# Query stage of a Perceiver kernel: two heads' 96-row half blocks packed into three blocks of 128

## The reference

```python
q_hk = (hidden_q @ Wq.T).reshape(Bv, Sv, H, K)
q_big = jnp.einsum('bshk,hkq->bshq', q_hk, w_kc_q)      # 192 channels a head
q_big = _apply_rope(q_big, sin_q, cos_q)                # x * cos + _rotate_half(x) * sin
kv_r = _apply_rope(kv_c, sin_k[None], cos_k[None])
q_r = jnp.einsum('bshq,hqr->bhsr', q_big, W_qr)
k_r = jnp.einsum('bld,hdr->bhlr', kv_r, W_kr)
scores = jnp.einsum('bhsr,bhlr->bhsl', q_r, k_r)
```

## Time and profile before

| | us |
|---|---|
| median of 3 runs (lowest, highest) | 1953.88 (1947.71, 1959.5) |
| the profiled execution | 1954.76 |
| its span, first to last instruction | 1952.6 |
| query stage, first query product to last key product | 38.63 to 257.97 |
| TensorE busy over the span | 1719.2 (88%) |
| VectorE, ScalarE, GpSimd busy | 1164.5, 600.8, 552.0 |

### The profile page before, as it was taken

One profiled execution on the slowest core, in us unless ns is written; L12 is line 12 of the kernel. 1 busy time (PEld: TensorE's weight loads), 2 busy tenths in 40 slices (PEclk: granted clock), 3 DMA queues, 4 the chain that ended last, 5 costly groups with the idle time before them and its releaser, 6 DMA issues. The chain is left out here.

```text
span 1952.6 us, 34931 instructions
## 1 busy us (share of the span) xinstructions
PE 1719.2 (88%) x14360; PEld 1174.4 (60%) x14360; DVE 1164.5 (60%) x1853; ACT 600.8 (31%) x997; POOL 552.0 (28%) x890
## 2 busy tenths in 40 slices
PE   3899968998995548999999999999999877999998
PEld 1333336886784226766776777766677665556555
DVE  4555557678764537676777767776677613443432
ACT  1111114334422313343444333433433311212212
POOL 1100014113211045444445554453554321000000
PEclk9899978999997869999999999998999978999999
DMA  6221120010000111111122111211211113200000
GB/s 200 84 59 47 49 52 1 1 33 12 1 1 3 33 30 31 43 37 39 37 48 47 39 42 36 48 41 35 47 36 43 26 23 113 87 0 0 0 0 21
DMA packets 150907, 74.47 MB, mean 38 GB/s; under 512 B 128176, under 2 KB 131504, under 8 KB 149488
## 3 DMA queue, kind: packets, MB, share of 16 engines
q1 hardware_dynamic: 150768, 72.48, 14.5%
HBM read 54.62 MB, written 17.83 MB: 37 GB/s over the span
## 5 line engine op out<-in xcount | busy, mean ns | idle before, releaser
L1604 DVE SCALAR_TENSOR_TENSOR acc<-PS,wc,acc 128x504 f32<-128x504 f32 (+2 forms) x384 | 281.5, 733 | 104.7 <-ACT acc L1388 95.5
L1158 PE MATMUL PS<-HT,wv 128*128 128x512 f32 x256 | 140.5, 676 | 8.3 <-DVE acc L1604 8.3
L1528 POOL TENSOR_TENSOR rr<-nm,con 128x16 f32<-128x16 f32 x16 | 46.4, 2901 | 341.1 <-DVE nm L1632 341.1
L1175 PE MATMUL PS<-wz,HT 128*128 128x256 f32 x512 | 123.6, 390 | 18.4 <-DVE acc L1604 17.0
L1388 ACT ACTIVATE acc<-PS,wc 128x512 f32<-128x512 f32 x128 | 87.7, 685 | 168.0 <-PE PS L1158 119.3
L1158 PE MATMUL PS<-HT,wkq 128*128 128x512 f32 x256 | 125.1, 614 | 11.4 <-DMA wkq<-in_gdn_w 8.5
L1614 DVE SCALAR_TENSOR_TENSOR y<-th,acc 128x512 f32<-128x512 f32 x128 | 93.3, 729 | 60.6 <-ACT th L1392 60.4
L1175 PEld LDWEIGHTS PS<-wz,HT 128*128 128x128 f32 x512 | 95.1, 192 | 40.8 <-DVE acc L1604 19.0
L1316 PE MATMUL PS<-wo,ogT 128*128 128x256 f32 x512 | 116.9, 387 | 1.1 <-ACT ogT L1440 1.1
L298 PE MATMUL PS<-HT,cw 128*96 128x512 f32 x256 | 117.5, 613 | 0.0
L1392 ACT ACTIVATE th<-acc 128x512 f32<-128x512 f32 x128 | 80.2, 626 | 116.8 <-DVE acc L1604 116.6
(11 more groups left out here) (228 smaller groups left out, 3357.6 us busy)
## 6 DMA issues: line engine op xcount, KB each, us to landing
a_rows<-AT SPq DMA_DIRECT2D x16, 512.0 KB, 2.6
wk<-in_l0x_k SPq DMA_DIRECT2D x16, 384.0 KB, 3.3
queries_scratch<-tts SPq DMA_DIRECT2D x32, 128.0 KB, 2.7
b<-queries_scratch SPq DMA_DIRECT2D x8, 512.0 KB, 5.0
wkq<-in_gdn_w SPq DMA_DIRECT2D x16, 256.0 KB, 3.2
wv<-in_gdn_w SPq DMA_DIRECT2D x16, 256.0 KB, 2.8
wz<-in_gdn_w SPq DMA_DIRECT2D x16, 256.0 KB, 2.9
wo<-in_gdn_w SPq DMA_DIRECT2D x16, 256.0 KB, 2.6
```

The lines of the kernel that those rows point to most:

```text
L1158: mm = pe.matmul(PS[:, QB[q], :], w[:, o:o + DK], HT[:, k, f * 512:(f + 1) * 512], start=(k == 0), stop=(k == DC - 1))
L1175: mm = pe.matmul(PS[:, ZB[m], w * 256:(w + 1) * 256], HT[:, k, n * P:(n + 1) * P], wz[:, k * 2 * DK:(k + 1) * 2 * DK], start=(k == 0), sto ...
L1604: v.scalar_tensor_tensor(a0, p0, wc[:, h % 2, 4 * c + 2 - k:4 * c + 3 - k], a0, ALU.mult, ALU.add).then_inc(s["conv"], 1)
```

## The change

Two heads are worked on as a pair (u). Of their 2 × 192 query channels, three blocks of 128 rows are made: block 0 holds channels 0 to 95 of the even head and 0 to 31 of the odd one, block 1 channels 96 to 191 of the even head and 96 to 127 of the odd one, and block 2 channels 32 to 95 and 128 to 191 of the odd head, its two halves one above the other. Blocks 0 and 1 are rotated as the two half blocks were. For block 2, ScalarE copies the two halves exchanged into `sw` (`swap`), and VectorE makes three further operations. The key product of a pair is one of three matmuls with 128 output rows, even head's in rows 0 to 63 and odd head's in 64 to 127; `mw` holds zeros where a block's rows belong to the other head, written once by GpSimd.

The two blocks are now one, `phase1`, without the barrier between them. `X` is loaded in two halves, the first ahead of `con`; the weights of heads 0 to 3 come early; the latent rotation is six pieces, one behind the rotations of each of the pairs 1 to 6; of the next stage's loads one or a few stand ahead of each pair. Nothing is a loop on the chip any more.

```diff
-    put("cosq", np.concatenate([cq[:, :HQ].T, cq[:, HQ:].T], axis=1))
-    put("sinq", np.concatenate([sq[:, :HQ].T, sq[:, HQ:].T], axis=1))
+    c0, c1, s0, s1 = cq[:, :HQ].T, cq[:, HQ:].T, sq[:, :HQ].T, sq[:, HQ:].T
+    k = HQ - 64
+    put("cosq", np.concatenate([np.concatenate([x, x[:k]]) for x in (c0, c1)] + [np.concatenate([c0[k:], c1[k:]])], axis=1))
+    put("sinq", np.concatenate([np.concatenate([x, x[:k]]) for x in (s0, s1)] + [np.concatenate([-s0[k:], s1[k:]])], axis=1))
...
-                    def queries(i, p, last):
-                        h = i * 2 + p
-                        pe.wait_ge(s["p1_cs"], h + 1)
-                        for f in range(2):
-                            for c in range(2):
-                                for k in range(DC):
-                                    mm = pe.matmul(PS[0:HQ, 2 + 2 * f + c, :], cw[:, p, k, c * HQ:(c + 1) * HQ],
-                                                   HT[:, k, f * 512:(f + 1) * 512], start=(k == 0), stop=(k == DC - 1))
-                            mm.then_inc(s[f"p1_q{f}"], 1)
-                        pe.wait_ge(s["p1_ms"], h + 1)
-                        for f in range(2):
-                            pe.wait_ge(s[f"p1_rope{f}"], h * 2 + 2)
-                            pe.wait_ge(s[f"p1_ts{f}"], h + 1)
-                            pe.matmul(PS[0:DCTX, 6 + f, :], mw[:, p, 0, :], r0[:, f, :], start=True, stop=False)
-                            pe.matmul(PS[0:DCTX, 6 + f, :], mw[:, p, 1, :], r1[:, f, :], start=False, stop=True).then_inc(s[f"p1_t{f}"], 1)
...
+    QT = HQ - 64
+    TILE_BANK = (2, 3, 2, 3, 5, 6, 5, 6)
...
+        cw = sb(ctx, "cw", [P, 2, DC, 3 * P])
+        mw = sb(ctx, "mw", [P, 2, 3, P])
...
+                def load(h):
+                    if h > 1:
+                        sp.wait_ge(s["wf"], h - 1)
...
+                def ahead(u):
+                    if u == 0:
+                        sp.dma_start(dn[:, :, :], d["ffn_dn"]).then_inc(s["next"], 16)
+                        sp.dma_start(wsd[:, :], d["ffn_wsd"].partition_broadcast(P)).then_inc(s["next"], 16)
...
+                    if u == 2:
+                        sp.dma_start(ug[:, :, :], d["ffn_ug"]).then_inc(s["ug"], 16)
...
+                half = TILES // 2
+                x = d["x"].rearrange("(n b) s c -> (b s) n c", b=2)
+                sp.dma_start(X[:, 0:half, :], x[:, 0:half, :]).then_inc(s["xa"], 16)
+                sp.dma_start(con[:, :], d["consts"]).then_inc(s["cons"], 16)
+                sp.dma_start(X[:, half:TILES, :], x[:, half:TILES, :]).then_inc(s["xb"], 16)
+                load(0)
+                load(1)
...
+                load(2)
+                load(3)
+                for u in range(PAIRS0):
+                    ahead(u)
+                    if u + 2 < PAIRS0:
+                        load(2 * u + 4)
+                    store(u, 0)
+                    if u + 2 < PAIRS0:
+                        load(2 * u + 5)
+                    store(u, 1)
...
+                    kr = wr[:, p, CQ:RW]
+                    if p == 0:
+                        for t in range(2):
+                            pe.matmul(PS[0:HQ, 1, t * DCTX:(t + 1) * DCTX], wr[:, p, t * HQ:(t + 1) * HQ], kr, start=True, stop=True)
+                    else:
+                        for t in range(2):
+                            pe.matmul(PS[HQ:P, 1, t * DCTX:(t + 1) * DCTX], wr[:, p, t * QT:(t + 1) * QT], kr, start=True, stop=True,
+                                      tile_position=(0, HQ))
+                        pe.matmul(PS[:, 1, 2 * DCTX:3 * DCTX], wr[:, p, 2 * QT:CQ], kr, start=True, stop=True)
...
+                def queries(u, f):
+                    if f == 0:
+                        pe.wait_ge(s["cs"], u * 3 + 3)
+                    if u == 0:
+                        pe.wait_ge(s["hT"], 4 * f + 4)
+                    else:
+                        pe.wait_ge(s[f"ts{f}"], u)
+                    for t in range(3):
+                        for k in range(DC):
+                            mm = pe.matmul(PS[:, qbank(f, t), :], cw[:, u % 2, k, t * P:(t + 1) * P],
+                                           HT[:, k, f * 512:(f + 1) * 512], start=(k == 0), stop=(k == DC - 1))
+                    mm.then_inc(s[f"q{f}"], 1)
+                def keys(u, f):
+                    if f == 0:
+                        pe.wait_ge(s["ms"], u * 3 + 3)
+                    pe.wait_ge(s[f"rope{f}"], u * 3 + 3)
+                    for t in range(3):
+                        mm = pe.matmul(PS[:, qbank(f, 0), :], mw[:, u % 2, t, :], rot[:, f, t, :], start=(t == 0), stop=(t == 2))
+                    mm.then_inc(s[f"t{f}"], 1)
+                pe.wait_ge(s["cons"], 16)
+                for t in range(4):
+                    turn(t)
+                fold(0)
+                fold(1)
+                pe.wait_ge(s["zero"], 1)
+                for u in range(PAIRS0):
+                    queries(u, 0)
+                    if u == 0:
+                        for t in range(4, 8):
+                            turn(t)
+                    queries(u, 1)
+                    if u + 1 < PAIRS0:
+                        fold(2 * u + 2)
+                    keys(u, 0)
+                    if u + 1 < PAIRS0:
+                        fold(2 * u + 3)
+                    keys(u, 1)
...
+                def swap(u, f):
+                    a.wait_ge(s[f"q{f}"], u + 1)
+                    if u > 0:
+                        a.wait_ge(s[f"rope{f}"], u * 3)
+                    x = PS[:, qbank(f, 2), :]
+                    a.activation(sw[0:64, f, :], x[64:P, :], ACT.Copy)
+                    a.activation(sw[64:P, f, :], x[0:64, :], ACT.Copy).then_inc(s[f"sw{f}"], 1)
...
+                for u in range(PAIRS0):
+                    if u == 0:
+                        for t in range(4, 8):
+                            keep_hT(t)
+                    swap(u, 0)
+                    swap(u, 1)
+                    if u + 1 < PAIRS0:
+                        folded(2 * u + 2)
+                    keep_keys(u, 0)
+                    if u + 1 < PAIRS0:
+                        folded(2 * u + 3)
+                    keep_keys(u, 1)
...
+                def rope(u, f):
+                    a, b, c = (view(PS[:, qbank(f, t), :]) for t in range(3))
+                    prod, done = s[f"prod{f}"], s[f"rope{f}"]
+                    v.wait_ge(s[f"q{f}"], u + 1)
+                    if u > 0:
+                        v.wait_ge(s[f"t{f}"], u)
+                    v.tensor_tensor(view(ra[:, f, :]), a, table("cosq", 0), ALU.mult).then_inc(prod, 1)
+                    v.tensor_tensor(view(rb[:, f, :]), b, table("sinq", 0), ALU.mult).then_inc(prod, 1)
+                    v.tensor_tensor(view(rc[:, f, :]), b, table("cosq", 1), ALU.mult).then_inc(prod, 1)
+                    v.tensor_tensor(view(rd[:, f, :]), a, table("sinq", 1), ALU.mult).then_inc(prod, 1)
+                    v.wait_ge(prod, u * 4 + 2)
+                    v.tensor_tensor(rot[:, f, 0, :], ra[:, f, :], rb[:, f, :], ALU.subtract).then_inc(done, 1)
+                    v.wait_ge(prod, u * 4 + 4)
+                    v.tensor_tensor(rot[:, f, 1, :], rc[:, f, :], rd[:, f, :], ALU.add).then_inc(done, 1)
+                    v.wait_ge(s[f"sw{f}"], u + 1)
+                    v.tensor_tensor(view(re[:, f, :]), c, table("cosq", 2), ALU.mult).then_inc(s[f"last{f}"], 1)
+                    v.tensor_tensor(view(rf[:, f, :]), view(sw[:, f, :]), table("sinq", 2), ALU.mult).then_inc(s[f"last{f}"], 1)
+                    v.wait_ge(s[f"last{f}"], u * 2 + 2)
+                    v.tensor_tensor(rot[:, f, 2, :], re[:, f, :], rf[:, f, :], ALU.add).then_inc(done, 1)
...
+                for u in range(PAIRS0):
+                    rope(u, 0)
+                    rope(u, 1)
+                    if 1 <= u <= 6:
+                        latent(u - 1)
...
+    order = np.concatenate([np.arange(k), HQ + np.arange(k), np.arange(k, HQ), np.arange(HQ + k, CQ)])
+    kcq, qr = g["L0_xattn_w_kc_q"].copy(), g["L0_xattn_W_qr"].copy()
+    kcq[1::2], qr[1::2] = kcq[1::2][:, :, order], qr[1::2][:, order, :]
```

357 lines of the change are left out of this document (173 added, 184 removed).

## The result

| | before | after |
|---|---|---|
| median (lowest, highest), runs | 1954.83 (1947.71, 1959.5), 4 | 1868.57 (1866.65, 1875.42), 4 |
| ratio, 95% interval | | 0.9569 [0.9545, 0.9593] |
| profiled execution, its span, mean granted clock | 1954.76, 1952.6, 0.941 | 1870.14, 1868.0, 0.944 |

The changed kernel is 86.3 us faster; the forecast was 1882, 71.3 us faster by its sum. Lines of the changed kernel: 279 transposes, 288 to 300 folds, 312 query product, 321 key product, 347 copies to `HT`, 380 and 381 swap, 415 `ug`, 421 to 433 norm, 445 to 457 rotation, 462 to 474 latent operations.

What follows compares the result with a forecast made beforehand. TensorE was taken to bound the query stage, busy 94% of 219.34 us. Terms −16.9 − 0.9 + 2.3 − 50.7 − 4.7 − 0.4 = −71.3 gave 1882 us, range 1869 to 1899.

Steps and rivals of the forecast that it cites:

- Start: Ahead of the first query product: queries start at 21.7 us in place of 38.63, 16.9 earlier.
- First slow passes: First query passes: half of the 1.8 us they took above full pace goes, a gain of 0.9.
- Transposes: Between the first two query products: four transposes with their copies to `HT` add 2.3 us.
- Pairs: TensorE's packed query stage: 19.46 us per pair of heads against 25.80, saving 50.7 over 8 pairs.
- VectorE's pace of 0.60: Rotations in the query stage: each VectorE operation costs 0.60 us, with 0.68 to 0.69 as the other bound.
- the margin of 0.2: Second rotation of a pair: ends at 11.4 us, TensorE wants it at 11.6, so hidden by 0.2 only.
- The rival of a VectorE-bound pair: Query stage: VectorE becomes a pair's bound, some 1 us a pair, 9 in all, giving 1891; chance 0.12.
- Narrow products: Rival on the odd fold: changes of column width cost 0.45 us more per pair, 4 in all, 1886; chance 0.05.
- `ug`: GpSimd's two products holding VectorE, now in pair 2: TensorE loses 5.7 us in place of 10.4, a gain of 4.7.
- End: Last pair of the query stage: takes 19.3 us, about as the others, a gain of 0.4.
- Loads and ScalarE: Query stage: weight loads and ScalarE's added copies are hidden behind other work and cost nothing.
- What follows the last product stays as it is: Behind the query stage's last key product: no change in time, so no term in the sum.

Runs made afterwards that it cites:

- the run with the start undone: Changed kernel with `con` ahead of an undivided `X`, all transposes and latent operations first, weights loaded late, packing kept: 1886.26 us, ratio 0.9681 to the kernel before.
- the added operation: Changed kernel with a tenth VectorE operation in each rotation, its result unread: 1879.88 us, ratio 0.9655 to the kernel before.
- the run with the weights behind: Changed kernel with the weights of heads 0 and 1 queued behind the latent inputs: 1883.44 us, ratio 0.9625 to the kernel before.
- the first group: Kernel before, unchanged (median 1944.34 us), beside three edits of the changed kernel on one chip, ratios 0.9567, 0.9681 and 0.9655.

## Why the prediction was right

Direction and mechanism held, and the stage's gain came out near its forecast (68.7 for 71.3). The total did so less well: 86.3 for 71.3, and the median of the changed kernel lies 0.4 us below the low end of the range. In part the stage's sum is luck: a start that came 2.0 better made up for `ug` (3.1 worse) and the end (1.3 worse) in part. Term by term, for the stage:

- **Start**, forecast −16.9, measured −18.9 (38.63 to 19.72). Two parts of the term were off. I had spaced the tiles by 1.41 as in the earlier trace rows; they came 1.06 apart: VectorE's work for a tile was all that stood between them, as the new order puts the next tile's statistics where it had waited for GpSimd's root. The halves of `X` don't matter for it: in the run with the start undone, where `X` is whole, the transposes are as close (11.61, 12.68, 13.74). And `con` released GpSimd at 7.14, not 7.6. Fold 0 began at 11.87 instead of 13.6. The run with the start undone puts 17.9 on this step less the transposes (its queries began 19.9 later and had no transposes between them, 2.1).
- **First slow passes**, −0.9, measured −0.3 (6.65 − 5.15 = 1.5 left of 1.8). Two more profiles of the same kernel had 1.2 and 2.0 left, so the term is within its scatter. They follow the first fold, not the clock time: in the run with the start undone 39.62 to 51.65 for two products is 12.03, again 1.7 above 10.30.
- **Transposes** +2.3, measured +2.1 (26.37 to 28.47).
- **Pairs** −50.7 at 19.46 a pair; measured 19.47, −50.6. The folds took 1.80 and 2.01 for 1.74 and 1.98, the key products 2.68 for 2.72. VectorE's pace of 0.60 held, and the margin of 0.2 was 0.26 by the added operation. The rival of a VectorE-bound pair was near: 0.26 over 18 operations is 0.014 us each.
- **Narrow products.** The odd fold with its further changes of mode took 0.21 more than the even one, and the two added passes alone were priced at 0.24. Both folds together took 0.09 more than their price, where this rival asked for 0.45, so it is refuted. The Trainium skill, TensorEngine Tiling (Array Packing), section "Key Properties", has a drain at each change of tiling mode; this trace shows none that costs a pair more than that 0.09.
- **`ug`**, −4.7, measured −1.6 (8.6 lost in the pair and 0.2 in the next one's queries, instead of 10.4). This is the term that was most mis-sized. I had the block reach rotation 0 and 1, with two waits of 2.6 and 3.1 and full clock. It reached rotation 1 alone, since `ug` landed as that rotation began, so the wait was one of 5.93 and the clock fell, 2.6 more for the six passes behind it. The forecast had the wait nearly right (5.7) and left the clock out of it. Whether two shorter waits would have kept the clock is not shown; behind the last pair's 2.62 it fell. In the run with the `ug` products moved the 8.6 of the pair were gone (7.3 at the last pass, as its first product was 0.6 slower and its last pair slower too). The rule that I had cited, of the Trainium skill, SBUF — State Buffer, section "SBUF: two separate sides", says that the engine that begins first keeps the port pair for its whole instruction. Both runs agree: the other's instruction stretches (4.98 on VectorE, 6.42 on GpSimd).
- **End**, −0.4, measured +0.9 (the last pair took 1.3 more than the others, the last head of before 0.4 more). The last key product began 16.54 us after the pair, as worked out (16.55), but behind the 2.62 us of waiting the last passes were slow, 4.21 in place of 2.7. I had left the clock out of a wait that I had in the sum.
- **Loads and ScalarE** at nothing: no pair shows a wait for weights or copies. The load order carries it, 9.3 us by the run with the weights behind.

Sum of the measured terms −68.4; the stage's end moved from 257.97 to 189.28, 68.7, so 0.3 are in none of them. Forecast was 71.3.

What the forecast did not have is the time behind the stage, "What follows the last product stays as it is". The work did; its time did not, by 17 us in the result and by nothing to 16 in the other packed versions. About 6 us came with the loops written out, on a chip of their own. **Still open:** the cause of this gain, why it differs between chips, and, if it is the clock, how the form of a program ahead moves it in loops 400 us later (where instructions lie and when they are fetched is one guess; no row shows it). The loops themselves, which are on the chip in all versions, were not written out.

## What to carry to other kernels

Where TensorE is the bound, fill the 128 columns before anything else: the saved passes and the waits that went (0.58 a head) gave the gain per pair to a hundredth of a us. The check to make first is whether the vector engine's longer chain still ends ahead of the product that needs it. Price a wait with the passes behind it at half pace as a likely bound, not by its length alone, and place bulk GpSimd work on SBUF where VectorE is idle. Measure on the chip how far two executions of the same kernel differ in a stage before reading a gain there: here 18.6 us in the loops.

## What was not expected of the hardware

- The same loops, with the same instructions, took 985.2 and 1003.8 us in two executions of one kernel. Before and changed differed in their median granted clock on two chips (0.938 and 0.941 on the second, 0.940 and 0.945 on the third); in the first group before had 0.943 and the packed versions 0.941 to 0.945.
- Writing out four loops of the query stage, and nothing else, gained 6.9 us by the medians (0.9958 [0.9938, 0.9979]), of which the stage itself shows about 1.
- The length of a wait alone doesn't tell whether the clock falls. Behind the last pair's 2.62 us the six passes took 4.16 to 4.54 in nine profiles of packed versions, but 2.84 in one (the changed kernel on the third chip), and 2.84 also behind 3.22 us in the run with the tenth operation. Behind a wait of 1.65 us ahead of the last head's second key product some passes were slow in two profiles of the kernel before and none in the written-out one. None were behind 0.87.

```profile
186.07 2.84 PE L321 MATMUL PS<-rot,mw 128*128 128x512 f32 x6 [2.62 <-DVE rot L457]
```

- The passes behind the first folds were slow in every profile, wherever the start stood (queries at 19.72, 29.19 or 39.62; the first product took 6.29 to 7.61 us in place of 5.15), though the profile notes a granted clock of 1.00 there.
